# Two transformer layers on one core: a second attention whose softmax weights are transposed one step later, ahead of the norm, with the stages in front of the scores one step sooner

## What is computed

```python
Q = (x @ Wq.T).reshape(b, s, h, hd)      # 16 heads of 16
K = (x @ Wk.T).reshape(b, s, h, hd)
V = (x @ Wv.T).reshape(b, s, h, hd)
scores = jnp.einsum('bshd,bstd->bsht', Q, K) / math.sqrt(hd)
attn = jax.nn.softmax(scores, axis=-1)
out = jnp.einsum('bsht,bstd->bshd', attn, V).reshape(b, s, dm)
...
h = _layernorm(x, axis=-1) * (1 + ca) + sa
x = x + ga * _L1_attn_ref(h, ...)
h = _layernorm(x, axis=-1) * (1 + cb) + sb      # and logits = h @ Wg, for the experts
```

## Time and profile before

| | us |
|---|---|
| median of 3 runs (1053.33 to 1059.0) | 1055.56 |
| the profiled execution's own time | 1061.21 |
| its span | 1059.4 |
| PE busy in the span | 967.2 (91%) |
| DVE busy | 621.9 (59%) |
| ACT busy | 494.6 (47%) |
| POOL busy | 384.2 (36%) |

### The profile page before, as it was taken

How to read it: one execution, slowest core, us unless ns; L and a number is a source line. 1 busy time by engine, 2 the same in 40 slices (tenths; PEclk the granted TensorE clock), 3 DMA queues, 4 the chain that set the end, 5 groups by cost and what they waited for, 6 DMA issues and landing times. The chain is left out here.

```text
span 1059.4 us, 30142 instructions
## 1 busy us (share of the span) xinstructions
PE 967.2 (91%) x11213; PEld 829.8 (78%) x11214; DVE 621.9 (59%) x1448; ACT 494.6 (47%) x1343; POOL 384.2 (36%) x341
## 2 busy tenths in 40 slices
PE   6899999989999999999978999999767889999996
PEld 3466665889999999999956877777656878899995
DVE  3478877853544544544504687889985677344442
ACT  2556665404445445445346776776552440222221
POOL 0534334521222223222204454555651101455552
PEclk9999999999999999999999999999958999999998
DMA  9874561394222222221055655666421630444441
GB/s 338 248 297 133 141 226 41 112 376 114 91 84 90 89 88 88 82 93 59 17 117 94 110 121 136 146 132 122 97 71 46 239 140 16 154 133 138 132 134 34
DMA packets 133008, 135.58 MB, mean 128 GB/s; under 512 B 73868, under 2 KB 122126, under 8 KB 130724
## 3 DMA queue, kind: packets, MB, share of 16 engines
q1 hardware_dynamic: 121668, 90.80, 30.7%
q0 software_dynamic: 11232, 43.27, 12.6%
HBM read 96.21 MB, written 44.77 MB: 133 GB/s over the span
## 5 line engine op out<-in xcount | busy, mean ns | idle before, releaser
L1138 PE MATMUL psall<-rows 128*128 128x128 f32 x1872 | 223.6, 276 | 1.7 <-DVE rows L1201 1.7
L1138 PEld LDWEIGHTS psall<-rows 128*128 128x128 f32 x1872 | 216.9, 193 | 2.3 <-issue 2.1
L1103 POOL DMA_INDIRECT x<-ffn_rows,tok_i x78 | 82.5, 1058 | 241.2 <-DVE rows L1220 144.2
L1152 PE MATMUL psall<-whi,rows 128*128 x624 | 141.0, 379 | 0.0
L1201 DVE COPY rows<-wlo 128x2048 f32 (+2 forms) x78 | 74.1, 950 | 98.5 <-PE psall L1138 89.7
L1152 PEld LDWEIGHTS psall<-whi,rows 128*128 128x128 f32 x624 | 115.7, 190 | 14.1
L1458 DVE STREAM_TRANSPOSE whi<-whi 32x512 f32<-32x512 f32 x128 | 89.8, 701 | 9.0 <-POOL whi L1421 7.7
L279 PE MATMUL psall<-cst 128*128 128x128 f32 x714 | 89.7, 283 | 0.5 <-PEq L1341 0.5
L1260 ACT ACTIVATE rows<-psall,vs 128x128 f32<-128x128 f32 x312 | 84.9, 383 | 10.7 <-PE psall L1138 7.1
L1538 ACT ACTIVATE whi<-psall 32x512 f32<-32x512 f32 x128 | 75.2, 588 | 29.6 <-PE psall L1667 25.6
L279 PEld LDWEIGHTS psall<-cst 128*128 128x128 f32 x714 | 85.7, 197 | 0.9 <-issue 0.6
(11 more groups left out here) (252 smaller groups left out, 1681.6 us busy)
## 6 DMA issues: line engine op xcount, KB each, us to landing
ffn_rows<-mod_rows SPq DMA_DIRECT2D x2, 4096.0 KB
wlo<-in_W SPq DMA_DIRECT2D x2, 4096.0 KB, 17.3
whi<-in_w SPq DMA_DIRECT2D x5, 1024.0 KB
whi<-mod_rows SPq DMA_DIRECT2D x4, 1024.0 KB, 14.2
ffn_rows<-rows SPq DMA_DIRECT2D x8, 512.0 KB
ffn_rows<-x SPq DMA_DIRECT2D x8, 512.0 KB
wlo<-attn_rows SPq DMA_DIRECT2D x32, 128.0 KB, 3.4
v_turn<-wlo SPq DMA_DIRECT2D x32, 128.0 KB, 3.1
```

What stands on the lines that cost most here:

```text
L1103: eng.indirect_dma_start(xin[j % DEEP], None, src_d, bass.IndirectOffsetOnAxis(tok_i[:, j:j + 1].bitcast(U32), 0), bounds_check=T, oob_is_ ...
L1138: last = eng.matmul(b_up[t.par][f // 4][:, (f % 4) * P:(f % 4 + 1) * P], w_now[:, c, f * P:(f + 1) * P], inT[t.par][:, c * P:(c + 1) * P], ...
L1152: last = eng.matmul(b_dn[t.par][:, 0:D], hidT[t.par][:, f * P:(f + 1) * P], w_down[:, bass.ds(e, 1), f, :].rearrange("p o n -> p (o n)"), ...
```

## The change

Transposes (`turn_exp`) go one step behind the multiply (`normalize_exp`, which has a lag of its own now, 13), and with them all that follows goes one step later. `turn_n`, `values`, `store_v`, `queries_keys` and `load_v` go one step sooner; `scores`, maximum and exponential keep their steps. A fourth `sc` buffer is added. On DVE `turn_exp` goes ahead of `norm2` in the list, on ACT the second `compact` goes ahead of `keep_h1T`. The loop has 48 steps in place of 47.

```diff
-        sc = [cv(GR * 32).rearrange("p (g n) -> p g n", n=32) for _ in range(3)]
+        sc = [cv(GR * 32).rearrange("p (g n) -> p g n", n=32) for _ in range(4)]
...
-        LAG_N, LAG_V, LAG_VST, LAG_QK, LAG_VLD, LAG_S = 2, 3, 4, 6, 7, 10
-        LAG_MX, LAG_EX, LAG_ET, LAG_PV, LAG_Y = 11, 12, 13, 14, 15
-        LAG_XLD, LAG_ROW, LAG_X, LAG_H = 14, 16, 19, 20
+        LAG_N, LAG_V, LAG_VST, LAG_QK, LAG_VLD, LAG_S = 1, 2, 3, 5, 6, 10
+        LAG_MX, LAG_EX, LAG_MUL, LAG_ET, LAG_PV, LAG_Y = 11, 12, 13, 14, 15, 16
+        LAG_XLD, LAG_ROW, LAG_X, LAG_H = 15, 17, 20, 21
...
-                tile_steps([(LAG_ET, normalize_exp), (LAG_X, add_attention), (LAG_MX, mask_other), (LAG_MX, sub_max)])
+                tile_steps([(LAG_MUL, normalize_exp), (LAG_X, add_attention), (LAG_MX, mask_other), (LAG_MX, sub_max)])
...
-                tile_steps([(LAG_H, norm2), (LAG_ET, turn_exp), (LAG_X, stats_sum), (LAG_MX, max_scores), (LAG_EX, sum_exp),
+                tile_steps([(LAG_ET, turn_exp), (LAG_H, norm2), (LAG_X, stats_sum), (LAG_MX, max_scores), (LAG_EX, sum_exp),
                             (LAG_Y, gate_attention)])
...
-                        wait_some(eng, c_["et"], t - 2)
+                        wait_some(eng, c_["et"], t - 3)
...
-                tile_steps([(LAG_MX, compact((0, 1), False)), (LAG_N, shift_h), (LAG_V, keep_v), (LAG_EX, exps), (LAG_H, keep_h1T),
-                            (LAG_MX, compact((2, 3), True)), (LAG_QK, keep_qk), (LAG_PV, keep_oT), (LAG_H, keep_logits), (LAG_X, rstd2)],
+                tile_steps([(LAG_MX, compact((0, 1), False)), (LAG_N, shift_h), (LAG_V, keep_v), (LAG_EX, exps), (LAG_MX, compact((2, 3), True)),
+                            (LAG_H, keep_h1T), (LAG_QK, keep_qk), (LAG_PV, keep_oT), (LAG_H, keep_logits), (LAG_X, rstd2)],
```

More of the change, by code:

```diff
@@ L1409, in mask_other @@
                     eng.wait_ge(c_["comp"], t + 1)
-                    s3 = sc[t % 3]
+                    s3 = sc[t % 4]
                     eng.tensor_tensor(s3, s3, bc_mid(pair_mask, GR), ALU.add).then_inc(c_["msk"], 1)
@@ L1443, in max_scores @@
                     eng.wait_ge(c_["msk"], t + 1)
-                    eng.tensor_reduce(mx1[t % 2], sc[t % 3], AX.X, ALU.max).then_inc(c_["mx"], 1)
+                    eng.tensor_reduce(mx1[t % 2], sc[t % 4], AX.X, ALU.max).then_inc(c_["mx"], 1)
                 def sum_exp(t):
                     eng.wait_ge(c_["ex"], t + 1)
-                    ch.do(eng.tensor_reduce(rs1[t % 2], sc[t % 3], AX.X, ALU.add))
+                    ch.do(eng.tensor_reduce(rs1[t % 2], sc[t % 4], AX.X, ALU.add))
                     eng.reciprocal(rs1[t % 2], rs1[t % 2]).then_inc(c_["sm"], 1)
@@ L1457, in turn_exp @@
                         rows_q = slice(32 * q, 32 * q + 32)
-                        last = eng.transpose(ebd[t % 2][rows_q, :, 32 * q:32 * q + 32], sc[t % 3][rows_q])
+                        last = eng.transpose(ebd[t % 2][rows_q, :, 32 * q:32 * q + 32], sc[t % 4][rows_q])
                     last.then_inc(c_["et"], 1)
@@ L1534, in stage @@
                         eng.wait_ge(c_["ss"], t + 1)
-                        wait_some(eng, c_["et"], t - 2)
+                        wait_some(eng, c_["et"], t - 3)
                         for q in quads:
                             rows_q = slice(32 * q, 32 * q + 32)
-                            last = eng.activation(sc[t % 3][rows_q], b_s[rows_q, :, 32 * q:32 * q + 32], ACT.Copy)
+                            last = eng.activation(sc[t % 4][rows_q], b_s[rows_q, :, 32 * q:32 * q + 32], ACT.Copy)
                         if done:
@@ L1544, in exps @@
                     eng.wait_ge(c_["sub"], t + 1)
-                    eng.activation(sc[t % 3], sc[t % 3], ACT.Exp, scale=HD ** -0.5).then_inc(c_["ex"], 1)
+                    eng.activation(sc[t % 4], sc[t % 4], ACT.Exp, scale=HD ** -0.5).then_inc(c_["ex"], 1)
                 def keep_oT(t):
```

## The result

| | before | changed |
|---|---|---|
| median of 4 runs, us | 1055.26 | 1078.72 (1078.33 to 1084.16) |
| ratio to before, 95% interval | 1 | 1.0201 (1.0172 to 1.023) |
| the profiled execution's span, us | 1059.4 | 1076.5 |
| DVE busy, us | 621.9 | 608.7 |
| PE busy, us | 967.2 | 974.5 |

The change makes the kernel 2.0% slower (the quotient of the two medians alone is 1.022, inside the interval); forecast was no change, and the measured time lies 10 us above the range. The medians differ by 23.5 us, the two profiled executions by 17.1, mostly because that of before (1061.21) lies 6.0 above its median. So the traces account for 17.1 of the 23.5. VectorE did lose work, 13 us of it, and the time still grew.

The account below looks back on a forecast made before the run. It took a ring of turn, copy, picks, mask, maximum and norm to close in one 6.80 us step, with VectorE nearly full. Terms +1.0 + 1.1 + 1.3 - 5.2 + 3.7 gave +1.9 us: 1057.5, range 1046 to 1069.

Parts of the forecast that it names:

- The round: Four steps in mid-stage, the fourth also projecting: 6.3, 7.9, 7.7 and 9.9 us, sum 31.8 against 30.9.
- both new waits: TensorE waits 1.6 us for the norm in a round's second step, 1.0 for L1561's bank in the third.
- a middle round under 0.95: Sign of a wrong forecast: granted clock under 0.95 in a round in the middle of the stage.
- Point 6, `load_norm`: SP's queue: the load loses one step of lead; the 6 us or more left cover its landing of 3.4.
- Point 2, the norm against the mask: VectorE's norm after the transposes takes 0.92 us instead of 1.72, plus 0.2 where it meets GpSimd's mask.
- last rival: VectorE not relieved: norm at 1.72 us beside the mask, +0.8 in each of six rounds, 1062 to 1064; chance 0.12.
- First round, +1.1: First round after the first project step: 31.9 us (5.4 + 8.9 + 7.7 + 9.9) against 30.8.
- The 8.9 us step: Second step of that first round: 8.9 us, as the first has no norm and leaves more of the ring's 14.2.
- the third rival, the clock: Closer waits bring a half-clock stretch per round in five rounds: 10 to 14 us slower, 1065 to 1071; chance 0.20.
- To the last scores, -5.2: From the last full round to the last scores: six steps, 43.0 us plus 2 for half clock, 45 against 50.2.
- Tail, +3.7: One more step of transposes, norm and turn ahead of tile 24's turn: 4.5 us less 0.8 saved on VectorE.

Follow-up runs that it names:

- e2: The changed kernel with the load of the normed rows issued one step sooner: 1073.69 us, ratio 1.0154 to the kernel before.
- e7: The changed kernel with six dummy matmuls ahead of TensorE's wait for the norm in the second step of a round: 1075.38 us, ratio 1.0199.
- e1: The changed kernel with the norm ahead of the transposes on VectorE again: 1063.97 us, ratio 1.0048 to the kernel before.
- e6: The changed kernel with all but the split and fourth buffer undone (old VectorE and ScalarE order, old lags ahead of the scores): 1064.21 us, ratio 1.0107.
- e5: The kernel before with turns, values, their store and load, queries and keys one step sooner: 1069.53 us, ratio 1.0121.
- e9: The kernel before with second picks ahead of the copy, turns to keys and normed-row loads sooner, keep_qk last on ScalarE, no split: 1052.28 us, ratio 0.9942.

## Why the prediction was wrong

The forecast failed in three of its terms: the start of the first scores (put at nothing, measured +5.1), the first round (+1.1, measured +6.5), and what follows the last full round (-5.2 and +3.7, measured -2.0 and +6.1). Behind them stand two steps of the mechanism, a load taken to be covered by its lead and a norm taken to cost at most 0.2 us more where it meets the mask, and the clock, for which the sum had only 2 us.

- *The round.* Right for two of the three. 31.8 was forecast, 31.33 measured at full clock; each step within some 0.2, and both new waits in their places (1.46 for the norm, 1.21 for L1561, forecast 1.6 and 1.0). The norm at 0.48 and 0.48 in middle rounds was forecast as well. The third round took 32.34, at a granted clock of 0.89, and the prediction had named a middle round under 0.95 as a sign of being wrong. That the three came to +0.8 in sum, near the forecast +1.3, is partly luck: the three of before held a slow step too.
- *Point 6, `load_norm`.* Wrong, 5 us. "The 6 us or more that are left cover its landing of 3.4" counted the landing and not the queue ahead: at the head the load stands in SyncE's list behind the four copies of keys, which themselves wait for L1530. It was issued at 552.98 for a turn that TensorE was ready for at 552.4. e2 took the wait away. The sum has no term for the time up to the first scores.
- *Point 2, the norm against the mask.* The 0.2 was wrong where the mask starts first: L1484 took 0.94 more at 627.68, and 1.00 and 0.99 more at 727.65 and 759.03. The Trainium skill's page "SBUF — State Buffer" (on the shared port pair) says that of two such operations the one that starts second waits for the whole of the first; in the first round the mask came 0.12 us sooner and the norm waited for its end, and in the middle rounds the norm came first and a mask took 1.50 instead of 1.27. The trace agrees with the rule to some 0.2 us: L1484 ended 0.28 after the mask's end, which is less than a whole norm of 0.48. The forecast had considered only a norm that starts first. Its last rival did price a slow norm in the second step, at 0.8 a round in each of six; it came in three steps, and cost more by the clock that fell behind it.
- *First round, +1.1.* Wrong, it was +6.5. The 8.9 us step became 10.87 and the step behind it 11.12 instead of 7.7. That is the third rival, the clock, in this round and not in every one: the two middle rounds with waits of 1.46 and 1.21 us kept full clock. e7 shows 5.1 us of it to be the clock, and in e1, without the long wait for the norm, this round kept 1.00. Later rounds of e1 did not (0.95, 0.95 and 0.89), so the late norm is not the only thing that lowers the clock.
- *To the last scores, -5.2.* It was -2.0. The steps took 5.6, 9.9, 6.6, 11.7, 7.1 and 7.4 us, where 5.9, 7.8, 6.1, 9.6, 5.8 and 7.8 had been forecast for full clock. Only the first ran at full clock throughout. The second holds the norm against the mask (1 us of the wait of 5.30). For the rest 2 us for half clock was too little: granted 0.67 over the stretch. With the norm first it takes 44.3 (e1), under the 45 that were forecast for a late norm.
- *Tail, +3.7.* It was +6.1 to tile 24's turn. In the tail TensorE waits for three of four norms (2.44, 3.54 and 3.13), and the norm stands behind the transposes in each of these steps, not in one. Over the longer stretch to the last project step, e1 puts the norm's place at 3.8 us, and e6 the extra step at 5 with the old order on ScalarE (3 with the picks ahead).
- *The form of the forecast.* Six terms of up to 5 us with opposite signs were added to 1.9, and 0.20 was left for the clock as one rival for all rounds. Head and tail, where steps are short and queues are not yet in their rhythm, were carried over from the steady round.

## What to carry over

When a stage is moved sooner in a lock-step schedule, follow each transfer's issue in its queue, at the first batch too: here what delayed it was the order ahead of it, more than its landing. A step's order on an engine decides which ring closes: open the ring by taking the waiting operation out of it (the picks, 0.6 to 0.7% faster with one line) before adding a buffer and a step, and keep what another engine waits for ahead of work that nobody waits for yet. When two engines' instructions come near each other, check which starts first in the first round and in the last, where neighbours are missing and the order turns round. Where waits move or grow, look at the granted clock of every round, not of one.

## What the runs showed of the hardware

- A VectorE norm with two inputs in SBUF and a GpSimd addition did not share: the norm that came 0.12 us later took 1.42 us instead of 0.48 (1.48 and 1.47 where it came 0.06 later).
- With TensorE idle for 3.14 us the granted clock fell to the lower level (0.63 over 6 us); with 1.6 us of dummy matmuls and 1.61 us idle in the same place it stayed at 1.00. The length of one wait does not decide it: waits of 1.46 and 1.21 us in a round left 1.00 in the changed kernel and went with 0.90 in e2, and a wait of 1.21 in e5 went with 1.00 in one project step and with 0.87 in two.
- In e1 one weighing (L1646) broke off in the middle of its matmuls with 1.44 us of idle that the profile puts on nothing:

```profile
667.78 0.80 PE L1646 MATMUL psall<-whi,wlo 128*32 128x64 f32 x41
...
670.01 0.54 PE L1646 MATMUL psall<-whi,wlo 128*32 128x64 f32 x23 [1.44 <-issue]
```

Such breaks came to 4.6 us in this line in e1 and to 2.0 to 3.3 us in e5, e7 and e9, and to 0.8 in the changed kernel. What releases them wasn't tried.
